# Stacked high and low parts for the delta products of a selective scan, one delta*u buffer, and newly dealt slots

## The reference

```python
u, res = split(x @ W_in, 2)
u = silu(conv3(u))
dt, Bm, Cm = split(u @ W_x, [16, 32])          # 16 + 16 + 16 columns
delta = softplus(dt @ W_dt + b_dt)             # 512 inner channels
dA = exp(delta * A);  dBu = (delta * u) * Bm   # for each of 16 states
h = dA * h + dBu;  y = sum over states of h * C
y = (y + u * D) * silu(res);  out = y @ W_out
```

## Time and profile before

| | |
|---|---|
| median of 3 runs | 2394.99 us (2393.97 to 2395.58) |
| profiled execution | 2394.69 us, of it the span of instructions 2392.8 us |
| block's scans, first to last | 25.2 to 1562 us; then routing and experts |
| a chunk in the middle | 95.40 us (odd, chunk 7), 95.86 us (even, chunk 8) |
| busy over the span | PE 94%, DVE 90%, POOL 77%, ACT 73% |

### The profile page before, as it was taken

The page is one execution under the profiler, slowest core; times in us unless marked ns, Lnnn a source line. Parts: engine busy times, 40 slices in busy tenths (PEclk is TensorE's granted clock), DMA queues, the critical chain, the costliest instruction groups (busy, mean ns, idle before and its releaser), DMA issues. The chain is left out here.

```text
span 2392.8 us, 39513 instructions
## 1 busy us (share of the span) xinstructions
PE 2245.3 (94%) x14183; PEld 1809.9 (76%) x14183; DVE 2145.2 (90%) x2917; ACT 1746.1 (73%) x2935; POOL 1851.2 (77%) x1028
## 2 busy tenths in 40 slices
PE   9999999999999999999999997745999999999995
PEld 5677777777777777777777766634999999999995
DVE  6999999999999999999999999986787787787775
ACT  6989989999899999998998998842344344434355
POOL 5899999999999999999999999952336437436465
PEclk9999999999999999999999999966999999999998
DMA  3222222222122222221222211122122322322353
GB/s 114 63 62 72 72 80 71 72 71 81 62 72 72 80 71 72 71 81 62 72 72 80 72 63 62 62 71 75 32 67 45 87 65 45 88 64 44 89 200 135
DMA packets 88722, 178.93 MB, mean 75 GB/s; under 512 B 9152, under 2 KB 51904, under 8 KB 88528
## 3 DMA queue, kind: packets, MB, share of 16 engines
q1 hardware_dynamic: 73648, 154.11, 19.4%
q0 software_dynamic: 14880, 22.29, 5.2%
HBM read 140.20 MB, written 36.18 MB: 74 GB/s over the span
## 5 line engine op out<-in xcount | busy, mean ns | idle before, releaser
L1105 DVE TENSOR_TENSOR_SCAN hst<-da,dbu 128x512 f32<-128x512 f32 x1008 | 1173.4, 1209 | 15.5 <-ACT da L806 10.1
L612 POOL TENSOR_TENSOR dbu<-du,b_all 128x2048 f32<-128x2048 f32 x254 | 1154.5, 4546 | 22.3 <-DVE hst L1105 22.3
L806 ACT ACTIVATE da<-delta,a_neg 128x512 f32<-128x512 f32 x1008 | 695.3, 699 | 101.4 <-DVE hst L1105 96.1
L2447 PE MATMUL gu<-x_part,w_part 128*128 128x384 f32 (+1 forms) x2304 | 485.8, 360 | 3.1 <-DVE x_part L2194 1.7
L2447 PEld LDWEIGHTS gu<-x_part,w_part 128*128 128x128 f32 x2304 | 402.9, 189 | 34.1 <-issue 4.5
L1272 PEld LDWEIGHTS hd<-ident,hst 128*128 128x128 f32 x2040 | 240.3, 141 | 187.3 <-issue 121.2
L772 ACT ACTIVATE hTC<-w,c_tok 128x512 f32<-128x512 f32 x510 | 350.1, 687 | 18.1 <-PE w L1272 12.8
L1190 PE MATMUL gen<-xT,w_u 128*128 128x512 f32 x720 | 360.9, 597 | 0.1
L1272 PEld LDWEIGHTS w<-ident,hst 128*128 128x128 f32 x2040 | 243.2, 141 | 142.9 <-issue 97.3
L1272 PE MATMUL hd<-ident,hst 128*128 128x128 f32 x2040 | 312.9, 276 | 35.9 <-DVE yacc L991 27.3
L991 DVE SCALAR_TENSOR_TENSOR yacc<-hd,c_tok,yacc 128x512 f32<-128x512 f32 x457 | 335.0, 733 | 12.6 <-PE hd L1272 7.6
(11 more groups left out here) (348 smaller groups left out, 2829.3 us busy)
## 6 DMA issues: line engine op xcount, KB each, us to landing
b_all<-b_rows SPq DMA_DIRECT2D x128, 512.0 KB, 3.7
xT<-in_xT SPq DMA_DIRECT2D x16, 514.0 KB, 5.0
xT_r<-in_xT SPq DMA_DIRECT2D x16, 512.0 KB, 5.0
x_rows<-in_x SPq DMA_DIRECT2D x16, 512.0 KB, 3.8
w_raw<-in_wg SPq DMA_DIRECT2D x8, 1024.0 KB, 5.0
w_raw<-in_wu SPq DMA_DIRECT2D x8, 1024.0 KB, 8.3
w_raw<-in_wd SPq DMA_DIRECT2D x8, 1024.0 KB, 10.7
x_dram<-x SPq DMA_DIRECT2D x15, 512.0 KB, 3.0
```

The costliest lines, as they stand in the source:

```text
L612: nc.gpsimd.tensor_tensor(dbu[DBU[n]][:], du[parity][:], b_n, ALU.mult).then_inc(dbu_ready, 1)
L806: nc.scalar.activation(da_bank[t % 2][:], delta[parity][:, t, :], ACT.Exp, scale=a_neg[:, t, n:n + 1]).then_inc(da_ready, 1)
L1105: nc.vector.tensor_tensor_scan(hst[DBU[n]][:, t, :], decay[:], dbu[DBU[n]][:, t, :], 0.0, ALU.mult, ALU.add).then_inc(scanned, 1)
L2447: last = nc.tensor.matmul(gu_bank[n % 2][i][:, 0:width(n)], gu_part[wp][:, i, kk, f * P:(f + 1) * P], x_part[xp][:, kk, tokens_of(j)], sta ...
```

## The change

The d products become a single pass each. ScalarE copies all 128 rows of `xd` to `xdT`, and `w_x` holds the 16 dt columns twice more, so that dt stands in three groups of rows; `w_dt` likewise. In each chunk VectorE masks `xdT` to its high bits after slot 27, GpSimd subtracts at n = 9 (the low parts), ScalarE copies the high parts over the first 64 rows at slot 30, and one matmul of `w_split` with `x_split` sums high*high, high*low and low*high. The weights are split the same way once, in chunk 0. There is one `du` buffer, which is filled after state 15's `dbu` is done, at the end of the chunk; state 15's `dbu` is made in four pieces, each of which waits for one scan. `c_tok` keeps the C columns only. Chunk 14 stashes two states more. The slot tables are dealt anew. The first chunk's own d products stay as they were. The diff, cut:

```diff
-    "cT": (0, 27), "u0": (1, 24, 29, 30, 32, 33, 34), "d0": (0, 28), "d1": (0, 32), "d2": (0, 35),
-    "u1": (1, 36, 39, 39, 40, 41, 43), "d3": (0, 38), "u2": (1, 45, 47, 47, 47, 48, 49), "ud0": (0, 45),
+    "cT": (0, 27), "u0": (1, 25, 28, 28, 31, 34, 34), "d0": (0, 30), "d1": (0, 33), "d2": (0, 36),
+    "u1": (1, 36, 39, 41, 42, 43, 43), "d3": (0, 37), "u2": (1, 45, 46, 47, 47, 50, 50), "ud0": (0, 45),
...
-EXP_AT = (42, 47)
-LN_AT = (49, 50)
-NORM_AT = (39, 43, 45, 49)
+EXP_AT = (45, 46)
+LN_AT = (48, 51)
+NORM_AT = (40, 43, 44, 49)
...
-SMALL_AT = 11
+SMALL_AT = 9
 ADD_AT = 15
-DU_AT = 15
...
+MASK_AT, HIGH_AT, LOW_AT = 27, 30, 9
...
-STASH[CHUNKS - 2] = {5: "w0", 6: "w1"}
+STASH[CHUNKS - 2] = {5: "w0", 6: "w1", 12: "w2", 14: "w3"}
...
-FIRST_EXP_AT = (43, 46)
-FIRST_LN_AT = (48, 50)
+FIRST_EXP_AT = (43, 45)
+FIRST_LN_AT = (47, 50)
...
-        du = [sb(f"du{i}", [P, DT, CL]) for i in range(2)]
+        du = sb("du", [P, DT, CL])
+        held = sb("held", [P, 2, CL])
+        w_split = sb("w_split", [P, DI], F32R)
+        x_split = sb("x_split", [P, CL], F32R)
...
+        masks = [tmp[:, i, :].bitcast(I32) for i in range(2)]
...
+            twice = w_x[:, :, XD:XD + 2 * RANK].rearrange("p k (i r) -> p k i r", i=2)
+            nc.gpsimd.tensor_scalar(twice, w_x[:, :, 0:RANK].rearrange("p k (i r) -> p k i r", i=1).to_broadcast(
+                [P, DT, 2, RANK]), 1.0, None, ALU.mult).then_inc(diag_ready, 1)
...
-                    if n == DU_AT and s.front:
+                    if n == LOW_AT and s.front:
+
+                        if not s.close:
+                            pool.wait_ge(dt_masked, 1)
+                            nc.gpsimd.tensor_tensor(w_split[:], w_dt[:], masks[1].bitcast(F32), ALU.subtract
+                                                    ).then_inc(dt_low, 1)
+                        pool.wait_ge(dt_masked, c + 2)
+                        nc.gpsimd.tensor_tensor(x_split[:], xdT[:], masks[0].bitcast(F32), ALU.subtract
+                                                ).then_inc(dt_low, 1)
+                    if n == NST - 1 and s.front:
...
-                        pool.wait_ge(u_ready, c + 2)
-                        nc.gpsimd.tensor_tensor(du[other][:], delta[other][:], u[:], ALU.mult).then_inc(du_ready, 1)
...
+                        if n == NST - 1:
+                            for t in range(DT):
+                                pool.wait_ge(scanned, c * SLOTS + DT * done + t + 1)
+                                ins = nc.gpsimd.tensor_tensor(dbu[DBU[n]][:, t, :], du[:, t, :], b_n[:, 0, :], ALU.mult)
+                            ins.then_inc(dbu_ready, 1)
...
+                if s.front:
+
+                    if s.main:
+                        pool.wait_ge(dbu_ready, (c + 1) * NST)
+                    pool.wait_ge(u_ready, c + 2)
+                    nc.gpsimd.tensor_tensor(du[:], delta[other][:], u[:], ALU.mult).then_inc(du_ready, 1)
...
-                    last = nc.scalar.activation(xdT[0:XD, :], bank[0:XD, :], ACT.Copy)
+                    last = nc.scalar.activation(xdT[:], bank[:], ACT.Copy)
...
+                    if slot == HIGH_AT and s.front:
+
+                        if not s.close:
+                            act.wait_ge(dt_low, 1)
+                            for rows in (slice(0, 32), slice(64, 128)):
+                                last = nc.scalar.activation(w_split[rows, :], masks[1][rows].bitcast(F32), ACT.Copy)
+                            last.then_inc(dt_high, 1)
+                        act.wait_ge(dt_low, c + 2)
+                        nc.scalar.activation(x_split[0:64, :], masks[0][0:64].bitcast(F32), ACT.Copy).then_inc(dt_high, 1)
...
+                    if slot == MASK_AT and s.front:
+                        dve.wait_ge(gate_ready, c + 1)
+                        if not s.close:
+                            dve.wait_ge(late_in, N_LATE * 16)
+                            nc.vector.tensor_scalar(masks[1], w_dt[:].bitcast(I32), HIGH_BITS, None, ALU.bitwise_and
+                                                    ).then_inc(dt_masked, 1)
+                        dve.wait_ge(ring_read, s.nth_read("xd") + 1)
+                        nc.vector.tensor_scalar(masks[0], xdT[:].bitcast(I32), HIGH_BITS, None, ALU.bitwise_and
+                                                ).then_inc(dt_masked, 1)
...
-                    last = nc.tensor.matmul(bank[:], w_dt[:, j * P:(j + 1) * P], xdT[:], start=True, stop=True)
+                    if j == 0:
+                        pe.wait_ge(dt_high, c + 2)
+                    last = nc.tensor.matmul(bank[:], w_split[:, j * P:(j + 1) * P], x_split[:], start=True, stop=True)
```

More of the change, by code:

```diff
@@ L273, in attention @@
         delta = [sb(f"delta{i}", [P, DT, CL]) for i in range(2)]
-        du = [sb(f"du{i}", [P, DT, CL]) for i in range(2)]
+        du = sb("du", [P, DT, CL])
+        held = sb("held", [P, 2, CL])
+        w_split = sb("w_split", [P, DI], F32R)
+        x_split = sb("x_split", [P, CL], F32R)
         xdT = sb("xdT", [P, CL])
-        c_tok = [sb(f"c_tok{i}", [P, LT, XD]) for i in range(2)]
+        c_tok = [sb(f"c_tok{i}", [P, LT, NST]) for i in range(2)]
         yacc = [sb(f"yacc{i}", [P, LB, DI]) for i in range(2)]
@@ L304, in attention @@
                       for i in range(N_TAPS * KD)})
+        stash.update({f"v{i}": held[:, i, :].rearrange("p (t q) -> p t q", q=P) for i in range(2)})
         stash.update({f"x{i}": xT[:, i, 0:CL].rearrange("p (t q) -> p t q", q=P) for i in range(KD)})
@@ L389, in attention @@
         tops = {}
-        for buffer, names in ((delta[0], TOP_WIDE[:4]), (du[0], TOP_WIDE[4:])):
+        for buffer, names in ((delta[0], TOP_WIDE[:4]), (w_r, TOP_WIDE[4:6]), (xT_r, TOP_WIDE[6:])):
             flat = buffer[:].rearrange("p t c -> p (t c)")
@@ L1147, in _ @@
             pe.wait_ge(weights_in, N_WEIGHTS * 16)
+            pe.wait_ge(diag_ready, 1)
             for t in range(DT):
@@ L1166, in _ @@
             for t in range(DT):
-                nc.tensor.matmul(lead_bank[f"d{t}"][:], w_dt[:, t * P:(t + 1) * P], xdT[:], start=True, stop=True
+                nc.tensor.matmul(lead_bank[f"d{t}"][:], w_dt[0:RANK, t * P:(t + 1) * P], xdT[0:RANK, :], start=True, stop=True
                                  ).then_inc(ring_full, 1)
```

63 lines of the change are left out of this document (36 added, 27 removed), and 16 rows, old and new, of tables (FILL_AT, FIRST_FILL_AT).

## The result

The changed kernel takes **2425.5 us** (median of 4 runs, 2424.3 to 2427.5) against 2394.6 us before: ratio 1.013, 95% interval 1.0119 to 1.0142. It is slower, inside the range and 5.5 us above the forecast. The profiled execution spans 2424.1 us, before 2392.8: 31.3 us more.

What follows compares the result with a forecast made beforehand. ScalarE's list, then GpSimd's chain, set each boundary: 1.99 us per even chunk, 1.51 per odd, seven each 24.5, plus chunk 0's 0.8: +25.3 on 2394.7, giving 2420 us; range for 8 in 10, 2388 to 2440.

Steps and rivals of the forecast that it cites:

- The bound: Chunk boundaries: VectorE paces to slot 35, ScalarE to the second logarithm, then GpSimd's chain to the next first scan.
- The logarithm, +1.18: Second logarithm one slot later, behind one decay and one scaling, so delta on GpSimd starts 1.18 us later per chunk.
- Four pieces, +0.42: State 15's dbu on GpSimd in four pieces: 4.96 us against 4.54, +0.42 a chunk.
- Splitting brings nothing: Claim that scans of slots 52 to 55 are all done before delta, so dbu 15's pieces gain nothing by waiting separately.
- The slack after odd chunks, -0.66: After odd chunks the next first scan could have started 0.66 us earlier, so that much added delay is absorbed.
- Slot 60 hardly waited: Claim that dbu 15 coming 4.5 us earlier, with du moved behind it, gains little at slot 60.
- Slot 31: Wait behind subtraction and ScalarE's copy at slot 30: +0.27 us in even chunks, +0.45 in odd ones.
- The mask, +0.33: VectorE's mask after slot 27: 0.42 us less 0.09 overlap, +0.33 a chunk, all on the path.
- the held rival: VectorE's mask stands still during GpSimd's multiply, some 2 us a chunk on the path: 2450 us, chance 0.10.
- TensorE's relief, -0.21: Single-pass d products save TensorE 3.1 us a chunk, of which only 0.21 (0 to 0.77) is credited.
- Slots 50 and 51 without waits: Sign expected in the profile after: VectorE's waits there, 0.30 for a turned state and 0.26 for a decay, disappear.
- Chunk 0, +0.8: First chunk pays pieces and two masks, 0.42 + 0.66, and idle time may shift: +0.8 us, from -2 to +3.

Runs made afterwards that it cites:

- with the old slots: Changed kernel (split products, one du buffer, four pieces) with every slot table of the kernel before, d products at 30, 33, 36, 38: 2410.1 us.
- 32-bit runs with and without them: Changed kernel with 32-bit d products over 16 rows: 2434.4 us keeping mask, subtraction and copy, 2429.7 us without them.
- the kernel before with short d products: Kernel before with its 32-bit d products over 128 of their 512 columns, output not the reference's: 2390.9 us, ratio 0.9986.
- the repairs: Changed kernel with second logarithm at slot 50, small instructions at n = 11 and dbu 15 in two halves: 2407.7 us.

## Why the prediction was right, point by point

**The bound.** Right. ScalarE's list and then GpSimd's chain set each boundary: delta starts 0.08 behind the second logarithm, the first scan 0.09 behind dbu 0, and moving the logarithm alone moves the time in both kernels.

**The logarithm, +1.18.** Right in place, and the largest term. In the changed kernel the logarithm ends 1.17 earlier when the slot is undone (77.06 against 78.23 after the chunk's first scan, chunk 7), and that returns 0.93 a chunk, since GpSimd is free only 0.89 (odd) to 1.03 (even) before delta. In the old kernel the same move costs 1.8: my price held only where the scaling that goes ahead finds its turn ready. The row that would have told it is one in the order, not in the times: behind which turn that scaling stands.

**Four pieces, +0.42.** The duration is right (4.97). "Splitting brings nothing" is wrong: I took the scans of slots 52 to 55 to be done before delta, and the fourth ends 1.49 us after it. Moving du behind dbu 15 is what makes dbu 15 early, and the pieces are what lets it start then. That the sum came out right here (+0.54 behind delta in the even chunk, forecast 0.42) is the duration being right, not the reason.

**The slack after odd chunks, -0.66.** Right for the new order (behind delta -0.11 in the odd chunk, forecast 0.42 - 0.66 = -0.24), for a reason that I had not seen. "Slot 60 hardly waited" was true only at the old time of the logarithm; the run with the logarithm moved in the kernel before waits 1.67 there. The changed kernel does not (0.15 in chunk 7, 0.21 in chunk 8).

**Slot 31.** Even chunks 0.23 (forecast 0.27). Odd chunks 0.65 to 0.92, forecast 0.45: mis-sized, and with chunk 0 the largest miss. The chain of fold, small instructions and subtraction was the right one. In chunk 7 it ends 2.97 behind the start of slot 28 (769.01 - 766.04) where I had 2.59; 0.29 of that is the fold, which takes 0.49 beside the mask in place of 0.20. That happens in three of the seven odd chunks (waits of 0.79 to 0.92); in the other four the fold takes 0.20 and the chain ends at 2.83 to 2.87, still late.

**The mask, +0.33, and the held rival.** The mask lasted 0.42 to 0.45 in every chunk: the rival did not happen, but its mechanism is real, and one slot earlier it costs 8.4 us. The margin in chunk 7 was 0.10 us (the multiply ends at 765.49, the mask starts at 765.59) where I had read 0.2, so that the mask stayed free in all seven odd chunks is in part luck. The Trainium skill, SBUF — State Buffer, section "Who interferes with whom", gives the rule cited in the prediction; the 1.98 us mask agrees with it. What the mask costs where it stands is read from its step: 0.45 (765.59 to the scan at 766.04), and 0.34 with the old slots (757.18 to 757.52); forecast 0.33. Removing mask, subtraction and copy with TensorE late (32-bit runs with and without them) returned only 0.47 per odd chunk and 0.03 per even one: VectorE then waited 0.37 and 0.35 for decays instead.

**TensorE's relief, -0.21.** Measured 0.25 in the old slots. In the new ones it is worth at most 0.67 a chunk; the wait of 0.45 at 788.48 that appears without it speaks for some. TensorE idles 2.5 us more in chunk 8, forecast 3. "Slots 50 and 51 without waits" was wrong in part: slot 51 has none, but two waits of the same size stand ahead of slot 47 (0.31) and of the turned state before slot 50 (0.27). GpSimd's chain ends later than VectorE's work at the boundary, so I take them to be harmless; no run removes them.

**Chunk 0, +0.8.** Mis-sized: +3.7, outside the -2 to +3 that I gave it. As far as the profiled executions go, 111.5 against 107.75, but with a granted clock of 0.72 and 0.86 from 64 to 76 us. With 1.00 there it lasts 109.6 in the changed kernel (two runs) and 106.3 in the kernel before with short d products: +3.3 at one clock. Two more products ahead of v0's last part delay the scan of slot 2 by 1.7, slot 31 waits 1.52 where it waited 1.00, and the first scan of chunk 1 waits 2.28 where it waited 0.27. I had treated its slots as noise.

**The sum.** 27.6 of the 31.3 us are chunks 1 to 14 (forecast 24.5), 3.7 are chunk 0. By first scans the seven even chunks lost 14.0 (forecast 13.9) and the seven odd ones 13.6 (forecast 10.6), so the miss is in the odd ones. Divided at delta's start:

| | forecast | measured |
|---|---|---|
| even, ahead of delta: 0.33 + 0.27 + 1.18 - 0.21 | 1.57 | 1.54 |
| even, behind it: 0.42 | 0.42 | 0.54 |
| odd, ahead of delta: 0.33 + 0.45 + 1.18 - 0.21 | 1.75 | 2.10 |
| odd, behind it: 0.42 - 0.66 | -0.24 | -0.11 |

The 0.35 too little ahead of delta in odd chunks is slot 31: with the small instructions moved back, odd and even chunks start delta alike (77.74 and 77.73). Of the 3.93 per pair, 2.32 are the two slots that the repairs take back, and 1.61 remain. With the old slots 1.71 remain, some 1.2 of it ahead of delta (split less relief, 0.59 a chunk where 0.33 + 0.27 - 0.21 = 0.39 was forecast) and 0.5 behind it (pieces and order). VectorE's timeline against that of the kernel before divides the 0.59 by place: 0.34 later at slot 28, behind the mask, 0.69 at slot 32, behind the copy, 0.57 at slot 44, behind the d products. Chunks 1 to 14 came out right by mechanism; the total missed by chunk 0 and slot 31, both forecast too small.
